# A gated cross-attention model on one core: heads in 32 rows each, 32-row tiles on TensorE, and both maxima of a unit in front of its eight score matmuls

## The reference

```
q = xn @ Wq (+ bq);  k = ctx @ Wk (+ bk);  v = ctx @ Wv (+ bv)      16 heads of 8 channels
scores = q_h @ k_h.T * scale                                       100 x 1444 per head
a1: keys whose mask is 0 get a score that leaves nothing of them (a row with nothing left is averaged)
a3: keys from a length on get -1e6
probs = softmax(scores);  out = concat_h(probs @ v_h) @ Wo (+ bo)
x = x + tanh(gate) * out
```

## Time and profile before

| | |
|---|---|
| time, median of 3 runs | 6736.84 us (6734.98 to 6741.63) |
| the profiled execution | 6736.52 us |
| its span | 6734.7 us |
| TensorE matmuls busy | 5947.1 us (88%) |
| TensorE weight loads busy | 4044.1 us (60%) |
| VectorE busy | 4732.6 us (70%) |
| ScalarE busy | 3471.3 us (52%) |
| GpSimd busy | 1972.7 us (29%) |
| mean granted TensorE clock | 0.938 |

### The profile page before, as it was taken

One profiled execution on the slowest core, in us unless ns is written; L12 is line 12 of the kernel. 1 busy time (PEld: TensorE's weight loads), 2 busy tenths in 40 slices (PEclk: granted clock), 3 DMA queues, 4 the chain that ended last, 5 costly groups with the idle time before them and its releaser, 6 DMA issues. The chain is left out here.

```text
span 6734.7 us, 123692 instructions
## 1 busy us (share of the span) xinstructions
PE 5947.1 (88%) x42776; PEld 4044.1 (60%) x42776; DVE 4732.6 (70%) x12652; ACT 3471.3 (52%) x5250; POOL 1972.7 (29%) x1415
## 2 busy tenths in 40 slices
PE   6999999969897999999999956768498799999996
PEld 4666666659894555555555545645388466566653
DVE  6878777867676666666666676634577777777775
ACT  3666666655553444444444433423255466666664
POOL 2222222224453222222222122334255222222220
PEclk9999999989997999999999977878699799999998
DMA  3333333220002333333333132356332333232321
GB/s 75 77 78 73 72 72 75 63 68 21 21 21 68 81 77 81 78 79 75 76 79 75 35 68 52 60 157 183 98 118 81 82 72 71 67 69 68 69 67 25
DMA packets 200964, 492.88 MB, mean 73 GB/s; under 512 B 31689, under 2 KB 135318, under 8 KB 199162
## 3 DMA queue, kind: packets, MB, share of 16 engines
q1 hardware_dynamic: 200386, 485.47, 29.5%
HBM read 270.18 MB, written 2.25 MB: 40 GB/s over the span
## 5 line engine op out<-in xcount | busy, mean ns | idle before, releaser
L850 PE MATMUL a_max<-a_stack,a_qblk 96*100 96x482 f32 (+1 forms) x4608 | 2003.5, 455 | 114.3 <-DVE a_mx L671 35.7
L550 ACT ACTIVATE a_probs<-a_scores 128x800 f32<-128x800 f32 (+1 forms) x1536 | 1281.3, 838 | 1019.0 <-PE a_scores L867 656.9
L863 PE MATMUL a_scores<-a_qblk,a_stack 128*128 128x400 f32 (+1 forms) x4608 | 1378.7, 372 | 8.1 <-POOL a_qblk L455 2.7
L665 DVE CUSTOM_DVE_ANT_0 a_dump<-a_max,a_mqf 100x482 f32<-100x482 f32 (+1 forms) x1536 | 978.5, 657 | 426.4 <-PE a_max L850 395.6
L850 PEld LDWEIGHTS a_max<-a_stack,a_qblk 96*100 96x100 f32 x4608 | 767.2, 167 | 745.1 <-issue 205.6
L671 DVE CUSTOM_DVE_ANT_0 a_dump<-a_max,a_penq 100x482 f32<-100x482 f32 (+1 forms) x1536 | 955.6, 657 | 280.9 <-PE a_max L850 261.7
L657 DVE TENSOR_REDUCE a_mx<-a_max 100x1 f32<-100x482 f32 (+1 forms) x1536 | 941.4, 654 | 257.6 <-PE a_max L850 239.8
L879 PE MATMUL a_pv<-a_probs,a_v_aug 128*32 128x200 f32 x18432 | 1051.8, 340 | 3.4 <-ACT a_probs L548 2.1
L863 PEld LDWEIGHTS a_scores<-a_qblk,a_stack 128*128 128x128 f32 (+1 forms) x4608 | 840.4, 186 | 185.6 <-issue 52.7
L1165 POOL TENSOR_TENSOR f_hb<-f_hb,f_wb 128x400 f32<-128x400 f32 x560 | 655.8, 1185 | 965.1 <-DVE f_hb L1413 490.2
L548 ACT ACTIVATE a_probs<-a_scores,a_kbias 128x800 f32<-128x800 f32 (+1 forms) x768 | 697.5, 926 | 413.6 <-PE a_scores L863 413.4
(11 more groups left out here) (302 smaller groups left out, 8471.7 us busy)
## 6 DMA issues: line engine op xcount, KB each, us to landing
a_stack<-a_khi SPq DMA_DIRECT2D x768, 180.5 KB, 3.4
a_ctxT<-in_ctxT_dram SPq DMA_DIRECT2D x128, 722.0 KB, 8.5
a_stack<-a_klo SPq DMA_DIRECT2D x384, 180.5 KB, 3.5
f_wb<-weights_by_token SPq DMA_DIRECT2D x24, 1600.0 KB, 10.7
f_wb<-weights_by_token SPq DMA_DIRECT2D x64, 400.0 KB, 6.3
a_ctxn<-in_ctxn_dram SPq DMA_DIRECT2D x32, 704.0 KB
a_mt_i<-in_mask1T_dram SPq DMA_DIRECT2D x32, 600.0 KB, 6.9
a_mq_i<-in_mask_dram SPq DMA_DIRECT2D x32, 564.1 KB
```

Source lines behind the costliest of these rows:

```text
L550: act.activation(out_, in_, ACT.Exp, scale=scale).then_inc(sc_free, 1)
L665: nc.vector.tensor_tensor_reduce(dump[:, k % 2, 0:n], src, mqf[:, b % 2, o:o + n], 1.0, -3.0e38, ALU.mult, ALU.max, out_).then_inc(mx_free, 1)
L850: pe.matmul(to[0:S, 0:n], qblk[0:96, b % 2, HALF * h + head, :], stack[0:96, b % 2, g, o:o + n], start=True, stop=True).then_inc(mx_full, 1)
L863: ins = pe.matmul(out_, stack[:, b % 2, 2 * h + g, kt * D:kt * D + r], qblk[:, b % 2, HALF * h + 4 * g:HALF * h + 4 * g + 4, :].rearrange( ...
```

## The change

Every head gets 32 rows of its own: on rows 0 and 1 the negated maximum in two parts against ones in `stack`, on row 2 the penalty of a3 (a row of `stack`, with a one from `q_row`), on 8 to 31 the head's 8 channels as hi, lo and hi. A group of `stack` then holds four heads in its four row groups. `qst` (three batches deep) replaces `qblk`, `qs` and `nsb`.

- A maximum is a matmul of 32 rows; the two of a unit use two neighbouring row groups, and both stand in front of the scores. Eight score matmuls of 32 rows, 128 keys and 100 columns replace the two of 400 columns; they alternate between the two row groups and their two banks. All 128 keys of the last tile are computed. In a1 the penalties stand first in the unit.
- LEAD is 24 units. The halves of a batch alternate in order from batch to batch.
- `q_proj` writes 128 rows; in a0 and a3 a one-row matmul (`q_row`) adds the bias or the one. `neg_turn` is four matmuls of 64 columns; VectorE adds their result to `qst` (`neg_rows`, 64 x 400) instead of copying 32 x 100.
- GpSimd no longer spreads the queries; it rounds them, forms the low part and adds (`q_parts`, three operations of 128 x 400), and splits the negated maxima (`neg_parts`, from VectorE).
- The keys go from `khi` and `klo` to DRAM (`k_store`) and from there into `stack`, four DMAs for each half (six in a3).
- In a3 VectorE reduces as in a0 and makes no penalty row, and the exponential has no bias.
- The side jobs move: OUT 2, NEG1 4, CONCAT 5, WO 8, Q 10, U 13, NEG0 15, K0 1, K12 3, V01 7, V2 9. `mask_rows` moves from unit 3 to 18.

```diff
-LEAD = 16
+LEAD = UNITS
+ROWS = 32
-        stack = sb("stack", [D, 2, GROUPS, KEYS], F32R)
+        stack = sb("stack", [D, 2, GROUPS, KT * D], F32R)
-        qblk = sb("qblk", [D, 2, HEADS, S], F32R)
+        qst = sb("qst", [D, 3, GROUPS, S], F32R)
...
-        OUT_AT, CONCAT_AT, WO_AT, NEG1_AT, U_AT, Q_AT, NEG0_AT = 2, 5, 8, 9, 13, 18, 21
-        V01_AT, V2_AT, K0_AT, K12_AT = 9, 11, 13, 15
+        OUT_AT, NEG1_AT, CONCAT_AT, WO_AT, Q_AT, U_AT, NEG0_AT = 2, 4, 5, 8, 10, 13, 15
+        K0_AT, K12_AT, V01_AT, V2_AT = 1, 3, 7, 9
...
+            def k_store(b):
+                sp.wait_ge(klo_ready, b + 1)
+                if b >= SLOTS:
+                    stack_there(sp, b - SLOTS, 0)
+                    stack_there(sp, b - SLOTS, 1)
+                for part, src in enumerate((khi, klo)):
+                    sp.dma_start(k_dram[b % SLOTS, :, :, part, :, :], src[:, :].bitcast(F32)).then_inc(k_out, 16)
...
-                for g in (2 * h, 2 * h + 1):
-                    for part, src in enumerate((khi, klo, khi)):
-                        sp.dma_start(stack[32 * part:32 * part + 32, b % 2, g, :].bitcast(F32),
-                                     src[32 * g:32 * g + 32, :].bitcast(F32)).then_inc(stack_in[b % 2][h], 16)
+                for r in (2 * h, 2 * h + 1):
+                    at, from_ = ROWS * r, k_dram[b % SLOTS, r]
+                    sp.dma_start(stack[at + 8:at + 24, b % 2, :, 0:KEYS].bitcast(F32),
+                                 from_.rearrange("g p i k -> (p i) g k")).then_inc(stack_in[b % 2][h], 16)
+                    sp.dma_start(stack[at + 24:at + 32, b % 2, :, 0:KEYS].bitcast(F32),
+                                 from_[:, 0].rearrange("g i k -> i g k")).then_inc(stack_in[b % 2][h], 16)
...
+            def q_parts(b):
+                taken(pool, "q", b)
+                scored(pool, b - 3, 1)
+                step(pool.tensor_copy(qh[:, :, :], qf[:, :, :]))
+                step(pool.tensor_scalar(ql[:, :, :], qh[:, :, :].bitcast(F32), low[:, 0:1], None, ALU.mult))
+                pool.tensor_tensor(qst[:, b % 3, :, :], qf[:, :, :], ql[:, :, :], ALU.add).then_inc(qst_ready, 1)
...
+            def neg_rows(b, j):
+                full(dve, "neg", 2 * b + j)
+                at = 2 * ROWS * half_of(b, j)
+                q_ = qst[at:at + 2 * ROWS, b % 3, :, :]
+                nc.vector.tensor_tensor(
+                    q_, p_ring("neg", 2 * b + j)[at:at + 2 * ROWS, 0:GROUPS * S].rearrange("p (g s) -> p g s", g=GROUPS),
+                    q_.bitcast(F32), ALU.add).then_inc(mx_free, 1)
...
-                    ins = pe.matmul(to[0:96, g * S:(g + 1) * S], wq[:, g, :], xnT[:, b * S:(b + 1) * S],
-                                    start=True, stop=True)
+                    ins = pe.matmul(to[:, g * S:(g + 1) * S], wq[:, g, :], xnT[:, b * S:(b + 1) * S],
+                                    start=True, stop=q_row is None)
+                    if q_row is not None:
+                        ins = pe.matmul(to[:, g * S:(g + 1) * S], q_row[:, g, :], ones_row[:, :], start=False, stop=True)
...
+                for g in range(GROUPS):
+                    ins = pe.matmul(to[at:at + 2 * ROWS, g * S:(g + 1) * S], nmsp[:, h, g, :].bitcast(F32),
+                                    ident[0:S, 0:S], start=True, stop=True)
...
-                pe.matmul(to[0:S, 0:n], qblk[0:96, b % 2, HALF * h + head, :], stack[0:96, b % 2, g, o:o + n],
+                at = ROWS * (2 * half_of(b, j) + r)
+                pe.matmul(to[0:S, 0:n], qst[at:at + ROWS, b % 3, g, :], stack[at:at + ROWS, b % 2, g, o:o + n],
                           start=True, stop=True).then_inc(mx_full, 1)
...
+                for r in range(2):
+                    at = ROWS * (2 * half_of(b, j) + r)
+                    ins = pe.matmul(to[:, r, g * S:(g + 1) * S], stack[at:at + ROWS, b % 2, g, kt * D:(kt + 1) * D],
+                                    qst[at:at + ROWS, b % 3, g, :], start=mask is None,
+                                    stop=mask is None or g == GROUPS - 1)
...
+                for i in range(2):
+                    pe.matmul(to[:, i, 0:4 * S].rearrange("p (h s) -> p h s", h=4), identb[:, :],
+                              bc(pen[:, b % 2, u % KT, :], 1, 4), start=True, stop=False)
...
+                    if mask is not None:
+                        penalty_mm(b, u)
                     max_mm(2 * g)
-                    score_mm(b, u)
+                    max_mm(2 * g + 1)
+                    score_mm(b, u, 0)
+                    score_mm(b, u, 1)
+                    score_mm(b, u, 2)
+                    score_mm(b, u, 3)
...
-                    max_mm(2 * g + 1)
```

More of the change, by code:

```diff
@@ new lines, in stack_load @@
+            def stack_load(b, j):
+                h = half_of(b, j)
+                sp.wait_ge(k_out, 32 * (b + 1))
+                scored(sp, b - 2, j)
+                if lens is not None and b == 0:
+                    sp.wait_ge(gone_out, 16)
+                for r in (2 * h, 2 * h + 1):
[4 more added lines that the diff above has]
+                                 from_[:, 0].rearrange("g i k -> i g k")).then_inc(stack_in[b % 2][h], 16)
+                    if lens is not None:
+                        sp.dma_start(stack[at + 2:at + 3, b % 2, :, 0:KEYS].bitcast(F32),
+                                     gone_dram[b:b + 1, :].unsqueeze(1).broadcast_to([1, GROUPS, KEYS]))\
+                          .then_inc(stack_in[b % 2][h], 16)
@@ L545, in exps @@
                 in_ = p_slot("exp", at)[0:rows, :, 0:4 * S]
-                if lens is not None:
-                    apart(act, passed["act"])
-                    act.activation(out_, in_, ACT.Exp, bias=kbias[0:rows, b:b + 1, kt], scale=scale).then_inc(sc_free, 1)
-                else:
-                    act.activation(out_, in_, ACT.Exp, scale=scale).then_inc(sc_free, 1)
+                act.activation(out_, in_, ACT.Exp, scale=scale).then_inc(sc_free, 1)
             def pen_make(b):
@@ L656, in reduce_max @@
-                if not special:
+                src, out_ = p_ring("max", k)[0:S, 0:n], mx[:, half_of(b, j), g, r, c:c + 1]
+                if b > 0 and k % (2 * KT) == 0:
+                    dve.wait_ge(nm_ready, 2 * (b - 1) + 1 - j + 1)
+                if mask is None:
                     nc.vector.tensor_reduce(out_, src, AX.X, ALU.max).then_inc(mx_free, 1)
@@ L758, in _ @@
                     g = UNITS * b + u + LEAD
-                    if u == 3 and b + 1 < B:
-                        mask_rows(b + 1)
                     maxima(g, 0)
+                    maxima(g, 1)
                     if b > 0:
@@ L2163, in host_layout @@
     L["ctxT"] = f["ctx_1024"].transpose(0, 2, 1)
-    rows = np.arange(D)
-    L["blk"] = np.concatenate([(rows[:, None] % 32 // DK == np.arange(4)), (rows[:, None] % 16 == np.arange(HEADS))],
-                              axis=1).astype(np.float32)
+    L["low"] = -(np.arange(D)[:, None] % 32 >= 24).astype(np.float32)
     def parts(w):
-        return np.stack([np.concatenate([w[:, 32 * g:32 * g + 32]] * 3, axis=1) for g in range(GROUPS)], axis=1)
+        out = np.zeros(w.shape[:1] + (GROUPS, 4, 32), w.dtype)
+        for r in range(4):
+            for g in range(GROUPS):
+                head = w[:, DK * (4 * r + g):DK * (4 * r + g) + DK]
+                out[:, g, r, 8:32] = np.tile(head, (1, 3))
+        return out.reshape(w.shape[:1] + (GROUPS, D))
     L["a0_wq"], L["a0_wk"], L["a0_wv"], L["a0_wo"] = (parts(f["L0_xattn_Wq"].T), f["L0_xattn_Wk"].T,
                                                      f["L0_xattn_Wv"].T, f["L0_xattn_Wo"].T)
-    L["a0_bq"] = np.stack([np.tile(f["L0_xattn_bq"][32 * g:32 * g + 32], 3) for g in range(GROUPS)], axis=1)
+    L["a0_q_row"] = parts(f["L0_xattn_bq"][None])
     L["a0_bk"], L["a0_bv"], L["a0_bo"] = f["L0_xattn_bk"][:, None], f["L0_xattn_bv"][:, None], f["L0_xattn_bo"][None]
```

344 lines of the change are left out of this document (160 added, 184 removed).

## The result

The changed kernel takes 8174.18 us (median of 4 runs, 8155.31 to 8186.94) against 6739.24 of the kernel before in the same runs: a ratio of 1.2125, 95% interval 1.2097 to 1.2153. Predicted were 6920, range 6550 to 7420. The sign was right, but by luck: the size and the cause were not what I forecast. I counted all work at 2.4 GHz, and TensorE is granted 1.2 GHz through most of a0 and a3.

What follows compares the result with a forecast made beforehand. TensorE was taken to set the pace, VectorE some 20 to 30% below. Terms a0 +96, a3 +10, a1 +35, prologues +45 made +186 on 6736.5, about 6920 us; range 6550 to 7420.

Steps and rivals of the forecast that it cites:

- all durations were taken at 2.4 GHz: TensorE in a0, a1, a3: busy 96 to 99% at granted clock 0.99, so all work was priced at 2.4 GHz.
- Maxima 0.23 for two: TensorE, each unit: two maxima in different row groups run at the same time, 0.23 us instead of 0.44.
- Scores 0.46 a unit, 0.112 a pair: TensorE, each unit: weight loads set the pace of eight 100-column scores, 0.112 us a pair, 0.46 against 0.37.
- rival 1: TensorE scores: row-tile loads hide behind each other, 0.24 a unit instead of 0.46; -368 us, 6555 us; chance 0.22.
- rival 2: TensorE scores: short rounded matmuls stream at fp32 rate, 0.168 a pair; +496 us, 7415 us; chance 0.16.
- rival 3: TensorE: row tiles do not overlap, +0.65 a unit, about +1490, 8400 us; chance 0.08.
- Plain pairs 2.40 in a0, 3.43 in a1: Job-free pairs of units: VectorE sets 2.40 us in a0, TensorE's work makes 3.43 in a1.
- Query projection over 3 us in a0: TensorE, a0 query projection: alternating full-array and one-row matmuls bring eight shape changes, +1.36 us; over 3 us in all.
- GpSimd off the path: GpSimd, 10.7 of 40.6 us busy: loses six spreading operations, gets three of about 1 us, counted as no cost.
- +35: Phase a1: +1.1 us a batch from the new layout and order, +35 us over the phase.
- Prologue +15 a phase: Start of each phase: eight more units of maxima +11, fewer at the end -3.5, way by DRAM +8; +45 us altogether.
- the sum of +186: Whole kernel: a0 +96, a3 +10, a1 +35 and prologues +45 us, added to the time before; chance 0.48.

Runs made afterwards that it cites:

- e19: Changed kernel, in a0 and a3 maxima on a constant tile over 128 rows, scores still 32-row tiles, VectorE adding the query row instead of one-row matmuls: 7365.75 us.
- e7: Changed kernel with VectorE adding a0's query bias and a3's penalty one in place of the one-row matmuls: 7774.23 us.
- e14: Kernel before, with a one-row matmul adding zeros behind each of the four query projection matmuls in a0 and a3: 6880.02 us.
- e17: Changed kernel with two zero matmuls before every unit of a0 and a3, VectorE adding in place of one-row matmuls, and `gone` ahead of `klo`: 7023.14 us.
- e11: Changed kernel with both maxima and scores of a0 and a3 on a constant tile over 128 rows, one-row matmuls kept: 8335.68 us.
- e3: Kernel before with maxima over 32 of their 96 rows, scores unchanged: 7767.98 us.
- e18: Changed kernel, in a0 and a3 scores on a constant tile over 128 rows, maxima still 32-row tiles, VectorE adding the query row instead of one-row matmuls: 9349.09 us.

## Why the prediction was wrong

- *The step that failed: all durations were taken at 2.4 GHz.* "TensorE is busy 96 to 99% at a granted clock of 0.99, so 2.4 GHz" was true of the kernel before and carried over unsaid; no term and no rival held a change of clock. The runs put 0.59 and 0.58 in its place in a0 and a3, and the maxima as 32-row tiles as the cause (the table), with rows and overlap not told apart.
- *Maxima 0.23 for two.* True at full clock, and better: they hide beside the scores. That price, the gain of the change, is what the clock took back: e19, with maxima over 128 rows at 0.44 for two, is 408 us faster than e7, which differs from it in the maxima alone.
- *Scores 0.46 a unit, 0.112 a pair.* Right: the pairs start 0.109 to 0.112 us apart in the trace, the second 0.15 behind the first; rival 1 (0.24) and rival 2 (0.7) are out, and so is rival 3.
- *Plain pairs 2.40 in a0, 3.43 in a1.* Measured 2.61 and 3.24 at full clock. The first missed the ring wait of 0.54 that two maxima ending together bring, the second that four row groups run at once: the two maxima hide beside the scores, and the change of shape, maxima and scores together take 0.59, where I had 0.17 + 0.23 + 0.46 = 0.86. In the other unit of the pair the ring takes 0.37 back.
- *Query projection over 3 us in a0.* Right, 3.1. Its switches of shape cost the 0.17 (e14: 142 us for 64 x 2.2).
- *GpSimd off the path.* Wrong in a1: its order put `gone` behind `klo`, which costs 231 us. I had counted its busy time and not what waits for each piece. Without that, a1 would have been 118 us faster than before (1596 against 1714), where I had +35.
- *Prologue +15 a phase.* Measured from the first key projection to the first P +39, +30 and +39. TensorE's rows in a0 show three DMA waits for the one that I priced:

```profile
85.47 1.12 PE L874 MATMUL a_max<-a_stack,a_qst 32*100 32x480 f32 x3 [22.11 <-DMA a_stack<-a_k_parts]
...
127.55 0.72 PE L874 MATMUL a_max<-a_stack,a_qst 32*100 32x480 f32 x2 [3.96 <-DMA a_stack<-a_k_parts]
...
135.45 1.94 PE L823 MATMUL a_scores<-a_ctxT,a_wk 128*128 128x480 f32 x2 [5.33 <-DMA a_ctxT<-in_ctxT_dram]
```

  The first maximum starts at 85.47, not 70.53: the way by DRAM costs 15 there, not 8. At the end the keys of batch 2 are wanted at unit 1, before their context has come. Inside the batches no wait for the stack's DMAs shows, as forecast.

At full clock the sum of +186 would have been too high, not too low. An estimate from e17: its batch of a0, 46.2, less the zero matmuls (0.88 a pair in six pairs, 0.45 in the six that go down to 2.60), plus 2.2 for the query rows, is 40.4 us, where I had 43.6; a3 likewise 40.0 where I had 43.1. That makes 0 us in a0, -88 in a3, -118 in a1 and +108 in the prologues, about 100 us faster than before. By this estimate all of the measured loss, and more, is the clock and the stall, and "slower" came true for a reason that the forecast did not have.

What stays open: why a fall at the one-row matmuls lasts 61.4 us in e11 and 3.4 us in the kernel before (e14), and why maxima over 32 rows cost the kernel before (e3) so much less of its clock than they cost e18. In e3 the two maxima of a unit do not overlap, and its scores take two loads a unit and not eight; neither was added to e3.

## What to carry to other kernels

Before the durations of a trace are added up for a changed kernel, ask whether the clock they were taken at will stand: here matmuls of 480 columns in 32-row tiles were cheaper each and cost TensorE nearly half its clock, and a little full-array work in between paid for itself. Of an engine that is hardly busy, read the order of its pieces and who waits for each, not its share. Two matmuls that end together need both of their ring slots free at once: here that was 0.54 us of wait in a pair of units.

## What the hardware showed

- Clock and busy time are separate: 100.00 of 100 us busy at 0.65, and 1646.10 of 1646.10 at 1.00.
- One change of tile shape costs 0.17 us at full clock: e14 and e3 show it again.
- Row tiles with different numbers of columns (480 and 100) in all four row groups start within 10 ns of each other (3367.55 in a1).
- A stall of 4.4 us on TensorE in each batch of a1 came with a clock of 0.91; without it 1.00.
- Work added to TensorE made the kernel faster four times: from 8174 to 7857 (zero matmuls), 7877 and 7896 (P twice, and P twice in even tiles) and, from e7's 7774, to 7366 (maxima over 128 rows).
- One-row matmuls added to the kernel before came with 15 falls of its clock, each 3.4 us long (e14); without them it has none in a0 and a3.
